# GpSimd's additions on ScalarE's groups: three levels in place of two, in an L1-attention transformer block

## What is computed

```python
def one_query(qs):
    return -jnp.sum(jnp.abs(qs[:, None, :, :] - k), axis=-1) * scale   # axis=-1: 64 numbers
...
a = jax.nn.softmax(a, axis=1)[:, :t]
```

## Time and profile before

| | |
|---|---|
| median of 3 runs | 3925.82 us (3923.77 to 3932.99) |
| the profiled execution's own time | 3925.79 us |
| its span in the trace | 3923.8 us |
| a steady iteration, from one load of `xin` to the next | 119.5 us |

### The profile page before, as it was taken

The page is one execution under the profiler, slowest core; times in us unless marked ns, Lnnn a source line. Parts: engine busy times, 40 slices in busy tenths (PEclk is TensorE's granted clock), DMA queues, the critical chain, the costliest instruction groups (busy, mean ns, idle before and its releaser), DMA issues.

```text
span 3923.8 us, 62787 instructions
## 1 busy us (share of the span) xinstructions
PE 3487.9 (89%) x15200; PEld 1807.2 (46%) x15200; DVE 3383.7 (86%) x4758; ACT 2720.3 (69%) x4801; POOL 2610.8 (67%) x2340
## 2 busy tenths in 40 slices
PE   5898989999889989889998899898899988998886
PEld 4444444444445444445444454444454444544433
DVE  4988889888888888888888888888888888988995
ACT  1677667767767767677676677676776776776774
POOL 2777666766666676667666666766677666667774
PEclk8989989999999999999998999999999999999998
DMA  1767666666666666666666666666667666667774
GB/s 54 148 128 140 126 125 136 129 138 128 126 137 134 131 135 127 130 130 129 137 132 123 136 133 131 137 125 130 131 132 139 131 127 134 133 131 139 139 148 85
DMA packets 192475, 508.47 MB, mean 130 GB/s; under 512 B 67990, under 2 KB 126230, under 8 KB 155448
## 3 DMA queue, kind: packets, MB, share of 16 engines
q0 software_dynamic: 73728, 469.79, 60.6%
q1 hardware_dynamic: 118712, 38.26, 4.8%
HBM read 10.79 MB, written 2.10 MB: 3 GB/s over the span
## 4 chain that ended last, share of the span: by engine, by line
PE 60%; DVE 11%; issue 10%; ACT 8%; DMA 5%; SPq 3%; POOL 1%; ACTq 1%; DVEq 0%; POOLq 0%
PE psU L367 31%; DVE S L754 7%; PE psC L380 6%; PE psZ L460 5%; DMA xin<-in_x 4%; PE psC L388 4%; PE psC L399 3%; ACT absd L559 3%; SPq L297 3%; PE psZ L437 2%; ACT kT L632 2%; PE psZ L501 2%; PE psZ L495 2%; PE psZ L454 1%; DVE S L765 1%
## 5 line engine op out<-in xcount | busy, mean ns | idle before, releaser
L754 DVE TENSOR_REDUCE S<-psU 128x16 f32<-128x1024 f32 x2304 | 2754.9, 1216 | 364.7 <-PE psU L367 343.7
L367 PE MATMUL psU<-flat,kT 99*128 99x512 bf16 x8192 | 2437.9, 404 | 247.4 <-DVE S L754 159.3
L559 ACT ACTIVATE absd<-psU 128x1024 f32<-128x1024 f32 x1792 | 1833.1, 1023 | 691.4 <-PE psU L367 678.1
L992 POOL TENSOR_TENSOR absd<-absd 128x1024 f32<-128x1024 f32 (+4 forms) x1024 | 1742.1, 1701 | 185.7 <-DMA absd<-absd 144.9
L367 PEld LDWEIGHTS psU<-flat,kT 99*128 99x128 bf16 x8192 | 743.3, 102 | 1348.7 <-DVE S L754 558.1
L976 POOL DMA_DIRECT2D absd<-absd x512 | 452.3, 883 | 632.1 <-ACT absd L559 593.5
L380 PE MATMUL psC<-c1in,w 128*128 128x256 f32 (+1 forms) x960 | 352.7, 456 | 20.1 <-DVE c1in L795 20.1
L399 PEld LDWEIGHTS psC<-c3in,w 128*128 128x128 f32 x1280 | 245.2, 206 | 164.7 <-DVE c3in L795 56.5
L399 PE MATMUL psC<-c3in,w 128*128 128x128 f32 x1280 | 274.2, 302 | 49.4 <-DVE c3in L795 49.4
L765 DVE TENSOR_REDUCE S<-absd 128x64 f32<-128x512 f32 (+2 forms) x512 | 311.3, 608 | 7.3 <-POOL absd L992 7.3
L460 PE MATMUL psZ<-P,v 128*128 128x256 f32 x1024 | 297.6, 383 | 0.8 <-ACT P L667 0.8
(11 more groups left out here) (127 smaller groups left out, 2468.1 us busy)
## 6 DMA issues: line engine op xcount, KB each, us to landing
absd<-absd POOLq DMA_DIRECT2D x288, 1024.0 KB, 7.7
absd<-absd POOLq DMA_DIRECT2D x192, 768.0 KB, 6.6
flat<-qparts SPq DMA_DIRECT2D x3072, 8.0 KB, 3.4
absd<-absd POOLq DMA_DIRECT2D x32, 512.0 KB, 4.8
xin<-in_x SPq DMA_DIRECT2D x32, 192.0 KB, 5.5
out_h<-result SPq DMA_DIRECT2D x32, 64.0 KB, 1.7
w<-in_w SPq DMA_DIRECT2D x1, 1280.0 KB
w<-in_w SPq DMA_DIRECT2D x1, 960.0 KB, 5.3
```

Of the source, the lines that this page charges most:

```text
L367: mm = nc.tensor.matmul(psU[:, slot % PLACES, hf], kT[0:99, b, hd, hf, :], flat[0:99, half % HALVES, :, lo:lo + 32], start=True, stop=True)
L559: nc.scalar.activation(absd[:, c % GROUPS, :, u], psU[:, slot % PLACES], ACT.Abs).then_inc(a_abs, 1)
L754: nc.vector.tensor_reduce(S[:, b, hd, SB * c:SB * c + SB], psU[:, slot % PLACES].rearrange("p a s w -> p s a w"), AX.XY, ALU.add, apply_ab ...
L992: nc.gpsimd.tensor_tensor(lo, lo, hi, ALU.add).then_inc(a_tree, 1)
```

## The change

The number of levels that GpSimd adds goes from two to three. The width that VectorE's last addition reads follows from it.

```diff
-LEVELS = 2
+LEVELS = 3
 WIDTH = 32 >> LEVELS
 TREE_AFTER = 10
 LAST_AFTER = 18
```

## The result

The changed kernel takes 3955.2 us (median of 5 runs, 3946.84 to 3966.66) against 3925.82 us before. The ratio is 1.0076, with a 95% interval of 1.0053 to 1.0098: 0.5 to 1.0% slower, where 3913 us was forecast, with a range to 3928. The profiled execution took 3946.84 us, with a span of 3945.0 us; it is the shortest of the five.

A forecast was written before the change was run, and what follows sets the result against it. TensorE was taken to bound most of an iteration, with VectorE full but not waited for. From 3925.79 us, -13.3 for steady iterations, -3.6 at the ends and +4 for GpSimd gave 3913 us; eight-in-ten range 3900 to 3928.

The forecast's parts named there:

- The prices of the instructions: VectorE's last addition at 408, 343 and 275 ns; GpSimd's third level 0.72 to 0.8 us for groups of four.
- the upper bound: GpSimd's third level would cost at most 568 us in all, if its time went by rows and not numbers.
- The place: At the iteration's turn, VectorE would wait about 0.7 us for chunk 13's tree, costed at nothing as covered.
- The two trees named: Trees of chunks 12 and 13 on GpSimd: third levels delay the issue between by 0.6 us and add 0.8 us.
- and the load was issued before: At the turn, everyone waits for xin, whose load was already issued, so VectorE's new wait was costed at nothing.
- the term for the turn: VectorE's wait for chunk 13's tree at each iteration's start: nothing, or 0.7 x 28 = 20 us without cover.
- The rival that ended slower: Chunk 13's tree ends 2.3 us later if rows of four cost like the second level: about 3947 us; chance 0.13.
- The gain: VectorE's shorter last additions: 14.8 us in steady iterations, taken at 0.9 as -13.3, and -3.6 at the ends.
- the three pieces of VectorE: Last additions in each steady iteration's chain, 0.54, 0.41 and 0.54 us, together gaining at most 0.53 us an iteration.
- nothing passes through: Time saved behind VectorE's three places goes back to matmuls or ScalarE; only the ends count: 3926 us, chance 0.16.
- The ends: Program's start and end: VectorE gains 3.6 us, and waits for GpSimd's trees lose 4 us.
- The signs of being wrong: Load distance stays, a new L992 enters the steady chain, or L765 in the chain moves to a formerly hidden place.

The follow-up runs named there:

- e5: The changed kernel, with VectorE's last addition of chunk 13's group 22 slots behind its end instead of 18: 3947.99 us.
- e1: The changed kernel's three levels everywhere except in the groups of chunks 12 and 13, which keep two: 3930.39 us.
- e2: The kernel before, with a third level only in the groups of chunks 12 and 13: 3955.84 us.
- e10: The kernel before (two levels), plus one GpSimd addition that nobody reads behind each tree of chunks 12 and 13: 3950.59 us.
- e11: The kernel before (two levels), but VectorE's last addition reads four of the eight numbers per sum: 3921.99 us.
- f3: e4 with two levels instead of three in the last two iterations: 3847.29 us.
- e4: The changed kernel (three levels everywhere), with the load of xin issued in the middle of the iteration ahead: 3858.98 us.
- e12: The changed kernel (three levels, all waited for), but VectorE reads eight numbers per sum as before: 3969.39 us.
- e13: The kernel before with early load of xin and three levels, but two in chunks 12 and 13 and in the last two iterations: 3798.76 us.

## Why the prediction was wrong, step by step

- **The prices of the instructions** were right to 1% on VectorE and to 3% on GpSimd, and so were both engines' busy times (3265 and 2970 us forecast, 3266.6 and 2951.5 measured). A slip in the upper bound did no harm: 568 us takes 0.45 us for the group of two, where that group's second level is 721 ns, which makes it 577; the 1260 ns for n = 4, taken from a line, stands in the trace as 1293. A number costs GpSimd (732 - 459) / 128 = 2.1 ns, about twice VectorE's. The Trainium skill, "GPSIMD Engine Reference", section 3.1, has nearly that ratio (1.96 for an add of 2048 numbers). That ratio didn't tell the outcome, as the prediction said.
- **The place** was right. The tree of chunk 13 is where VectorE waits, once an iteration, for about 1.1 us with 0.7 forecast, and most of that wait was covered by the wait for `xin` (e5). The two trees named are the two that cost (e1, e2).
- **The step that failed** is the half sentence "and the load was issued before", by which I took the cover as fixed. When a load is issued doesn't fix when it lands. GpSimd's DMA behind the late tree runs ahead of the load on the DMA engines, and the copy comes 7.4 us behind that DMA's issue. I had the issue at 2104.23 pushed back by 0.6 us in the sum, and didn't follow the one at 2115.75, which the same sum puts 1.4 us later (1.0 nearer to the load in the trace). So the term for the turn stood at nothing, and the two late trees measured 29 us (e2), 25 with the delay of GpSimd alone (e10). That the whole of it is the load's 1.0 us at each of 28 turns would fit the number too well: half of that shows in the iterations of the profiled runs, and part of the loss lies behind the last load. This mechanism was in none of the rivals. The rival that ended slower had the right tree with the wrong mechanism: it asked rows of four to be dear, and they aren't.
- **The gain** failed as well, as the term -13.3 of the sum. The chain had the three pieces of VectorE, and in the change's chain they are as short as forecast (0.34 and 0.27 us). But e11 measures the whole gain at 3 us, where 16.9 stood in the sum: of the 112 us that VectorE saved, 101 came back as its wait for TensorE's slots. That is the rival "nothing passes through", for the gain by itself. Which of the three pieces met the wait for `xin`, and which the lower clock, isn't shown.
- **The ends** were mis-sized. GpSimd stands in the chain there more often than I counted on: 8.6 us more from the last load to the end, where gain and loss were forecast to cancel (-3.6 + 4). f3 against e4 gives 12 to 16 us.
- **The signs of being wrong** were well chosen. A new L992 does stand in the chain of steady iterations, in four of them, and the distance of the loads grew from 119.6 to 120.1 us where 119.0 was forecast.

The sum as measured, in differences of medians: the cost alone is 44 us (e12), the gain in its presence 14 us (3969 to 3955), the rest 29 to 30 us. That the same shorter reads are worth 14 us with three levels and 3 us with two would fit the tree of chunk 13: there VectorE is late by 1.06 us, and what is read behind it counts. But the interval of e12 and that of the change are each some 8 us wide to either side, so that even the difference between 14 and 3 isn't shown.

## What to carry to other kernels

A wait that hides your new wait is only cover if nothing in the change can lengthen it: follow every DMA that the delayed engine issues, and ask which transfer comes behind it on the DMA engines, on whatever queue it was issued. That a piece stands in the chain doesn't say that shortening it pays; measure it with the gain alone (here: read half) before building on it. And a wait that stands in every iteration's chain can be worth more than its length: moving one load was worth 109 us, 3.6 us an iteration for a wait of 2.5, and over eight times what the change was forecast to give.

## What the runs showed of the hardware

- A load of 192 KB that SyncE's queue issued 0.76 to 1.75 us (medians) behind a 768 KB addition of GpSimd's queue was usable 7.4 us behind the addition's issue in both kernels; its last packet ended 0.3 to 0.6 us behind the addition's. Issued 0.55 us ahead of the addition, its packets were done after 2.0 us and it was usable after 3.1.
- GpSimd's additions on rows of four numbers cost what rows of eight do: 732 ns for 256 (most of them rows of four) against 721.
- VectorE's reduce from SBUF took 275, 343, 409, 543 and 674 ns for 128, 192, 256, 384 and 512 numbers read per partition, and 408 to 409 ns for 256 whether it wrote 32 numbers or 64.
- At the turn of the changed kernel's iteration TensorE's granted clock fell from 1.00 to 0.50, the lower level of 1.2 GHz, within 2005 to 2009 us, ahead of the copy of `xin`. TensorE had been busy 2.50 of the 4 us before. With the load early there were iterations at 1.00 throughout (e13). The same code at 0.99 took 117.1 us an iteration in the changed kernel and 121.4 at 0.91.
